# Attention scores of an MLA layer: from two to four column tiles with 32 keys each, turned by VectorE instead of TensorE

## What is computed

```python
q = rmsnorm(x @ wq_a.T + b) @ wq_b.T + b          # 16 heads, 128 + 64 (rope)
kv, k_pe = rmsnorm(...), rope(...)                # one latent key/value of 128, one rope key of 64, for all heads
scores = (q_nope @ wkv_b_k . kv + q_pe . k_pe) / sqrt(192)    # within a sequence of 64 tokens, causal
p = softmax(scores);  out = (p @ kv) @ wkv_b_v @ wo.T + b
```

## Time and profile before

| | us |
|---|---|
| median of 3 executions (1074.99 to 1075.48) | 1075.35 |
| span of the profiled execution, first to last instruction | 1073.7 |
| TensorE busy | 1052.0 (98%) |
| VectorE, ScalarE, GpSimd busy | 501.7, 340.6, 280.1 |
| granted TensorE clock, mean | 0.999 |

### The profile page before, as it was taken

One profiled execution on the slowest core, in us unless ns is written; L12 is line 12 of the kernel. 1 busy time (PEld: TensorE's weight loads), 2 busy tenths in 40 slices (PEclk: granted clock), 3 DMA queues, 4 the chain that ended last, 5 costly groups with the idle time before them and its releaser, 6 DMA issues.

```text
span 1073.7 us, 16794 instructions
## 1 busy us (share of the span) xinstructions
PE 1052.0 (98%) x6465; PEld 862.3 (80%) x6465; DVE 501.7 (47%) x914; ACT 340.6 (32%) x630; POOL 280.1 (26%) x329
## 2 busy tenths in 40 slices
PE   6999999999999999999999999999999999999997
PEld 3677786788888888888888888888888888888886
DVE  3666556545555544555555557442522251234114
ACT  3565545423222232123222234342222222223220
POOL 2433362321112111131111312232242123213412
PEclk9999999999999999999999999999999999999999
DMA  9999973200022000220013061600020002000101
GB/s 361 415 418 396 386 274 91 72 20 21 21 64 94 20 12 21 72 96 21 20 50 99 21 206 41 216 1 1 1 76 4 1 1 79 1 1 1 40 1 40
DMA packets 40755, 101.24 MB, mean 94 GB/s; under 512 B 6954, under 2 KB 11077, under 8 KB 36197
## 3 DMA queue, kind: packets, MB, share of 16 engines
q1 hardware_dynamic: 38948, 96.62, 25.3%
q10 hardware_dynamic: 1728, 3.54, 0.8%
HBM read 74.45 MB, written 17.30 MB: 85 GB/s over the span
## 4 chain that ended last, share of the span: by engine, by line
PE 96%; DVE 1%; issue 1%; DMA 1%; POOL 0%; ACT 0%; SPq 0%; DVEq 0%; POOLq 0%; ACTq 0%
PE b_z L44 8%; PE b_z L46 8%; PE b_z L45 8%; PE b_turn L44 5%; PE b_turn L46 4%; PE b_turn L45 4%; PE b_score L44 4%; PE b_score L46 4%; PE b_prob L46 4%; PE b_prob L44 4%; PE b_score L45 4%; PE b_prob L45 4%; PE b_read L46 4%; PE b_read L44 4%; PE b_read L45 4%; PE b_read L623 2%
## 5 line engine op out<-in xcount | busy, mean ns | idle before, releaser
L1516 POOL TENSOR_TENSOR f_hT_lo<-f_h,f_hT_hi 128x512 fp32r<-128x512 f32 x64 | 82.1, 1283 | 241.3 <-ACT f_hT_hi L1571 232.3
L1632 DVE TENSOR_TENSOR f_h<-f_h 128x512 f32<-128x512 f32 x64 | 45.4, 710 | 154.8 <-ACT f_h L1564 154.8
L816 POOL TENSOR_TENSOR m_sc<-m_sc,m_rs 128x1024 f32<-128x1024 f32 x16 | 30.5, 1908 | 248.5 <-DVE m_rs L979 248.5
L44 PE MATMUL b_z<-m_zT_lo,m_wq_hi 128*128 128x512 f32 x192 | 74.9, 390 | 0.3 <-issue 0.3
L46 PE MATMUL b_z<-m_zT_hi,m_wq_hi 128*128 128x512 f32 x192 | 74.7, 389 | 0.0
L45 PE MATMUL b_z<-m_zT_hi,m_wq_lo 128*128 128x512 f32 x192 | 74.7, 389 | 0.0
L987 DVE TENSOR_TENSOR m_x<-b_score,m_x 128x512 f32<-128x512 f32 x32 | 22.1, 691 | 97.3 <-PE b_score L46 97.3
L858 ACT ACTIVATE m_qT<-b_z,m_q_bias 128x512 f32<-128x512 f32 x64 | 44.1, 689 | 71.1 <-PE b_z L46 65.2
L806 POOL TENSOR_TENSOR m_qpe<-m_qpe,m_swapped 128x512 f32<-128x512 f32 x32 | 41.3, 1292 | 79.7 <-DMA m_swapped<-m_by_sin 79.7
L1571 ACT CAST f_hT_hi<-f_h 128x512 fp32r<-128x512 f32 x64 | 39.8, 622 | 52.4 <-DVE f_h L1632 52.4
L879 ACT ACTIVATE m_sc<-m_sc 128x512 f32<-128x512 f32 x32 | 20.2, 632 | 103.0 <-DVE m_sc L971 103.0
(11 more groups left out here) (280 smaller groups left out, 2863.9 us busy)
## 6 DMA issues: line engine op xcount, KB each, us to landing
x_ctx_in<-ctx_rows_dram SPq DMA_DIRECT2D x16, 1024.0 KB, 14.5
x_ctxT<-ctx_turned_dram SPq DMA_DIRECT2D x15, 1024.0 KB, 14.0
m_swapped<-m_by_sin SPq DMA_DIRECT2D x128, 64.0 KB, 2.0
m_raw<-attn_raw_dram SPq DMA_DIRECT2D x6, 768.0 KB, 10.6
m_z_in<-z_scratch SPq DMA_DIRECT2D x4, 1152.0 KB, 5.7
x_x_all<-x_dram SPq DMA_DIRECT2D x16, 256.0 KB, 14.7
m_x<-x_scratch SPq DMA_DIRECT2D x4, 1024.0 KB, 6.3
x_scratch<-m_x SPq DMA_DIRECT2D x4, 1024.0 KB, 4.3
```

The source lines that it names most:

```text
L44: nc.tensor.matmul(out, lh, rl, start=first, stop=False)
L816: q.tensor_tensor(e, e, rs[:].unsqueeze(2).broadcast_to([P, HB, SEQ]), ALU.mult).then_inc(s["normed"], 1)
L1516: q.tensor_tensor(hT_lo[k % 6][:], h[:, k % 2], hT_hi[k % 6][:].bitcast(F32), ALU.subtract).then_inc(s["h_lo"], 1)
L1632: v.tensor_tensor(h[:, k % 2], h[:, k % 2], h[:, k % 2], ALU.mult).then_inc(s["squared"], 1)
```

## The change

Scores are laid out with 32 keys on 32 partitions and four blocks of keys side by side: part c holds 2 sequences, its 128 tokens are cut in 4 tiles of 32. Bank b of the two score banks has one sequence of each part: block w = 0 is the first 32 queries on the first 32 keys, w = 1 the last 32 queries on the first keys, w = 2 the last on the last, so the quarter above the diagonal is no longer computed. A unit's scores are 128 x 768 instead of 128 x 1024. VectorE turns them with its own transpose of 32 x 32 blocks (`turn_scores`, `turn_probs`), TensorE's transposes go, and the mask is added after the turning, by GpSimd. Maximum and sum over 64 keys are now made of two blocks by two small instructions. `exp`, the copy of the probabilities and their split are one instruction each. The rope scores stand in two runs, the second behind `rope_half(u+1, 0)`. Token order changes with it: loads of z, loads and stores of x1 are 4 DMAs of 32 partitions where they were one.

```diff
     def load_z(sp, g):
-        sp.dma_start(z_in[:, :, 0:ZW], z_t[g]).then_inc(z_loaded, 16)
-        sp.dma_start(z_in[:, :, ZW:ZW + ROPE], z_t[g][:, :, QLR + KVLR:ZW]).then_inc(z_loaded, 16)
+        for c in range(PARTS):
+            sp.dma_start(z_in[part(c), :, 0:ZW], z_t[g, c]).then_inc(z_loaded, 16)
+            sp.dma_start(z_in[part(c), :, ZW:ZW + ROPE], z_t[g, c][:, :, QLR + KVLR:ZW]).then_inc(z_loaded, 16)
...
+        def mask(u):
+
+            pool.wait_ge(s["s_turned"], 2 * (u + 1))
+            own = sc[:].rearrange("p (b w n) -> p b w n", b=2, w=3)[:, :, 0::2]
+            q.tensor_tensor(own, own, causal[:].unsqueeze(1).unsqueeze(1).broadcast_to([P, 2, 2, HU * QB]),
+                            ALU.add).then_inc(s["masked"], 1)
...
         def slot(g, n, u):
             if runs(g, n, 1):
+                mask(u - 1)
+            rope_add(u, 0)
+            if runs(g, n, 1):
                 norm(u - 1)
-            rope_add(u)
+            rope_add(u, 1)
             if n == 1:
                 bias_x1(g)
...
         def exp(u):
 
-            for half in range(2):
-                act.wait_ge(s["shifted"], 2 * u + half + 1)
-                a.activation(sc[:, HALF * half:HALF * half + HALF], sc[:, HALF * half:HALF * half + HALF],
-                             ACT.Exp, scale=SCALE).then_inc(s["exped"], 1)
+            act.wait_ge(s["shifted"], u + 1)
+            a.activation(sc[:], sc[:], ACT.Exp, scale=SCALE).then_inc(s["exped"], 1)
...
+        def turn_scores(u):
 
             dve.wait_ge(s["scored"], u + 1)
...
+            for b in range(2):
+                v.transpose(sc[:, 3 * P * b:3 * P * b + 3 * P], b_s[b][:, 0:3 * P]).then_inc(s["s_turned"], 1)
+
+        def turn_probs(u):
+
+            dve.wait_ge(s["normed"], u + 1)
+            dve.wait_ge(s["pv"], u)
+            v.transpose(pT[:], sc[:]).then_inc(s["p_turned"], 1)
...
         def scores(g, u):
...
+            for b in range(2):
+                for k in range(2):
+                    for c in range(PARTS):
+                        t_.matmul(b_s[b][part(c), 2 * P * k:2 * P + P * k], keys_all[:, 0, 2 * b + k, c], queries(qT[:], b, k, c),
+                                  start=k == 0, stop=False)
+            rope_scores((0, 1)).then_inc(s["half_scored"], 1)
...
+        def rope_scores(heads):
+
+            for k in range(2):
+                for c in range(PARTS):
+                    for b, h in enumerate(heads):
+                        of = slice(SEQ * h, SEQ * h + SEQ)
+                        to = b_s[b][part(c), 0:3 * P].rearrange("p (w h n) -> p h w n", w=3, h=2)[:, h, 2 * k:2 + k]
+                        mm = t_.matmul(to, keys_all[of, 1, 2 * b + k, c], queries(qpe[of], b, k, c), start=False, stop=heads[0] == 1 and k == 1)
+            return mm
```

More of the change, by code:

```diff
@@ L795, in gpsimd @@
         pool.wait_ge(s["setup"], 1)
-        for half in range(2):
[L797 to L806, removed]
+        for c in range(PARTS):
+            rows = causal[part(c)].rearrange("p (h k) -> p h k", k=QB)
+            q.affine_select(out=rows, in_=rows, compare_op=ALU.is_ge, fill=-BIG, base=0,
+                            pattern=[[0, HU], [-1, QB]], channel_multiplier=1).then_inc(s["consts"], 1)
@@ L827, in groups @@
             slots(pool, slot)
-        return dict(groups=groups, rope_add=rope_add, norm=norm)
+        return dict(groups=groups, rope_add=rope_add, mask=mask, norm=norm)
     def scalar(act):
@@ L857, in q_part @@
             act.wait_ge(s["scored"], u)
-            a.activation(qT[:, h], b_q[h % 2][:], ACT.Identity,
+            a.activation(qT[:, 2 * (h % 2) + h // 2], b_q[h % 2][:], ACT.Identity,
                          bias=q_bias[:, HU * n + h:HU * n + h + 1]).then_inc(s["q_done"], 1)
         def probs(u):
[L862 to L865, removed]
+            act.wait_ge(s["p_turned"], u + 1)
+            act.wait_ge(s["pv"], u)
+            a.copy(pT_hi[:], pT[:]).then_inc(s["pT_hi"], 1)
         def out(u):
@@ L955, in mask @@
-        def mask(u):
+                split(of_part(oT_lo, c), b_o[c][:].rearrange("p (t h q) -> p t h q", t=T4, h=HU), of_part(oT_hi, c), s["oT_lo"])
+        def turn_scores(u):
             dve.wait_ge(s["scored"], u + 1)
[L958 to L961, removed]
@@ L1078, in rope_half @@
             for k in range(KQ):
+                if of is not None and k == KQ - 1:
+                    pe.wait_ge(s["half_scored"], of + 1)
                 mm = mm3(nc, b_r[m][:], (wq_hi[:, k, cols], wq_lo[:, k, cols]), (zT_hi[:, k], zT_lo[:, k]), k == 0, k == KQ - 1)
             mm.then_inc(s["rope_made"], 1)
-        def turn_scores(u):
-            pe.wait_ge(s["masked"], 2 * (u + 1))
-            for half in range(2):
-                turn(b_s[half], lambda k: sc[:, HALF * half + P * k:HALF * half + P * k + P], HB // 4).then_inc(s["s_turned"], 1)
         def q_unit(g, n, u):
@@ L1120, in project, with weigh @@
             mm.then_inc(s["projected"], 1)
-        def weigh(g, u, half, last=False):
+        def weigh(g, u, last=False):
             pe.wait_ge(s["kv_lo"], g + 1)
@@ L1195, in slot @@
                     pe.wait_ge(s["zq_lo"], T4 * (g + 2))
-                for half in range(2):
-                    weigh(before(1)[0], u - 1, half)
+                weigh(before(1)[0], u - 1)
             scores(g, u)
@@ L1202, in slot @@
             ahead = (g, n + 1) if n < 3 else (g + 1, 0)
-            rope_half(*ahead, u + 1, 0)
-            turn_scores(u)
+            rope_half(*ahead, u + 1, 0, u)
+            scores_end()
             rope_half(*ahead, u + 1, 1)
@@ L2065, in _ @@
             pe.wait_ge(F["s"]["xT_lo"], 4)
-            for half in range(2):
-                m["weigh"](G, U - 1, half)
+            m["weigh"](G, U - 1)
             m["scores"](G, U)
-            m["project"](2, U - 1, 0)
-            m["turn_scores"](U)
-            for i in range(1, 4):
+            m["project"](2, U - 1, 0, U)
+            m["scores_end"]()
+            for i in range(1, 3):
                 m["project"](2, U - 1, i)
             f["up"](0, 0)
-            m["turn_probs"](U)
             f["up"](0, 1)
-            m["weigh"](G, U, 0, last=True)
+            m["project"](2, U - 1, 3)
             pe.wait_ge(F["s"]["relu"], 2)
-            m["weigh"](G, U, 1, last=True)
+            m["weigh"](G, U, last=True)
             f["up"](0, 2)
```

215 lines of the change are left out of this document (109 added, 106 removed).

## The result

The changed kernel takes **1126.98 us** (median of 4 runs, 1124.36 to 1128.11), the kernel before 1075.41 beside it: a ratio of 1.0476, 95% interval [1.0461, 1.0491]. It is 4.8% slower; 1105 were forecast, 22 us too few. The profiled execution has a span of 1122.6 us, 48.9 more than the earlier trace rows.

What follows compares the result with a forecast made beforehand. TensorE bounds, busy 1052.0 of 1073.7 us. 1073.7 - 34 + 10 + 7 + 28 + 5 + 6 + 2 + 6 = 1103.7, with 1.7 around the span 1105 us, 2.8% slower; forecast 1088 to 1115 (64%), range 1088 to 1132.

Steps and rivals of the forecast that it cites:

- rival 2: TensorE: column tiles of 32 run only two at a time, 32 us, up to 1137; rivals 2 to 4 together 24%.
- rival 3: TensorE rope runs: short matmuls have a floor of 27 ns, 17 us, 1122; rivals 2 to 4 together 24%.
- rival 4: VectorE's transposes cost twice a pass, 13 to 16 us, 1120; rivals 2 to 4 together 24%.
- TensorE's saving, 16 units: Transposes 1.76 and latent scores 0.44 saved, rope scores 0.06 lost: 2.14 us a unit, 34 us.
- third head, ordinary units: TensorE's third head waits 1.25 us for the softmax chain and `q_part(0)`; 8 units, 10 us.
- third head, n=0 units: Split of new values adds 0.6 ahead of the chain: 1.85 us each in 4 units, 7 us.
- third head, three n=1 units: Groups 1 to 3: mask waits behind GpSimd's bias additions after the x1 reload; 9.2 us three times, 28 us.
- residuals (`x2_done`): Units n = 0: swap's DMAs behind eight z issues delay the first residual 2.4 us in two units, 5 us.
- late weight fill: Unit 0: third fill waits for a split behind the probabilities on VectorE, s + 23.3 against 17.3: 6 us.
- end of stage m: Where stage f is woven in, the same softmax chain costs about 2 us.
- clock: Matmuls behind long TensorE waits run at 1.2 GHz for a while: 1.5 us for each of 4, 6 us.
- rival 1: Reload does not hold the mask and the chain is cheaper: 1073 or 1065 us; 9% for faster, 3% within 0.2%.

Runs made afterwards that it cites:

- experiment 4: Kernel before, with the x2 store and the x1 reload each in four DMAs of 32 partitions in place of one; 1075.54 us, ratio 0.9999.
- experiment 7: Changed kernel with 52 matmuls that nobody reads put ahead of the third head's wait in each of three slots; 1119.08 us.
- experiment 3: Changed kernel with sums over keys and reciprocal ahead of the second half's rotation on VectorE again; 1115.77 us, ratio 1.0373.
- experiment 1: Changed kernel with the four bias additions to x1 one unit later in GpSimd's queue; 1089.85 us, ratio 1.0135.
- experiment 2: Changed kernel with the mask added by VectorE at the head of the shift, in place of GpSimd, bias additions left in place; 1100.14 us.
- experiment 8: Experiment 6 plus normalisation ahead of GpSimd's first-half rope addition and transposed probabilities ahead of VectorE's second-half rotation, last unit alike; 1051.18 us, ratio 0.9772.
- experiment 6: Changed kernel with the orders of experiment 1 and experiment 3, and the first query head evicted ahead of the exponential on ScalarE; 1069.33 us, ratio 0.9943.

## Why the forecast was right, and where it was short

The direction and the mechanisms that it priced held; sizes were off, and a cost that it set to nothing was there. The measured time lies above the 1088 to 1115 us to which the forecast gave 64%. It is inside the range up to 1132 only by the room left for rivals 2 to 4, none of which came true: so much of it is luck.

By term, in whole us of the profiled span: the forecast beside what was measured. Waits are taken from the start-to-start periods of the units, changed kernel against the kernel before, with the 2.2 us saved in each added back. So the sum comes out by construction; the split within a period goes by the waits and the clock in its rows.

| term | forecast | measured |
|---|---|---|
| TensorE's saving, 16 units | -34 | -35 |
| third head, ordinary units | +10 | +9 |
| third head, n=0 units | +7 | +7 |
| third head, three n=1 units | +28 | +37 |
| residuals (`x2_done`) | +5 | +8 |
| late weight fill | +6 | +7 |
| end of stage m | +2 | +5 |
| clock | +6 | +10 |
| step back of the group loop | 0 | +1 |
| sum | +30 | +49 |

**What TensorE saves**: right in each part, by the unit's first two microseconds and by the periods. Taking four tiles to cost per pass what two cost was the step that rivals 2 and 3 disputed.

**The ordinary unit's chain**: right, 1.1 to 1.3 us against 1.25. Transposes, mask (1.26), maximum, exponential (0.84) each came within 0.05 of their term.

**Unit n = 1**: the step that failed, by size. "That store and load are now four DMAs each I cost at nothing" was wrong, and the reason given for it too: the issues did not hide. The last of four stores is issued 1.75 us behind the first, and the reload, which waits for it, goes out that much later in experiment 4. In unit 9 store to addition went from 10.73 to 14.20 us; 9.2 + 3.5 is the 12.7 measured. Experiment 4 shows 2.3 of the 3.5 in a kernel that has nothing else of the change. The waits of groups 1 and 3 are 12.3 us, 3.1 over the forecast. In group 1 it is the same thing (10.57 to 13.82). In group 3 only half of it is (12.46 to 13.96): the kernel before was 1.7 us slower there than in unit 9, with its store issued at 576.17, and the forecast read unit 9 alone for all three. In all 10 us.

```profile
588.63 5.04 POOL L811 TENSOR_TENSOR m_x<-m_x,m_wo_b 128x512 f32<-128x512 f32 x4 [20.58 <-DMA m_x<-x_scratch]
```

**Units n = 0**: in the slot behind unit 4's scores (308.70) the rotation can start after 17.4 us, forecast at 16 to 17, and the residual starts after 24.7 and ends after 25.4, where the forecast had its end at 24.7:

```profile
326.06 0.75 DVE L952 SCALAR_TENSOR_TENSOR m_by_sin<-b_read,m_rope_bias,m_sin 128x512 f32<-128x512 f32 x1 [6.04 <-DMA m_swapped<-m_by_sin]
...
333.38 0.68 DVE L1015 TENSOR_TENSOR m_x<-b_score,m_x 128x512 f32<-128x512 f32 x1
```

So it costs 3.0 in two units, not 2.4, and 1.3 ahead of group 3, where I expected none since it loads no z. The end of stage m shows waits of 2.0 and 1.6 in the rows; from the last scores to the end of the span it took 437.9 us against 435.4, with 2.2 of saving in it, so 5 in all. Which work fills the last us of that was not tried.

**Clock**: the 4 falls at 1.5 us were in truth six: three long waits (5 us, by experiment 7), the two of 3 us (1.6 each, measured for one by experiment 3), the weight fill (an estimate of 1.6, half of its 3.2 us at half clock). My step "three of the new waits, and perhaps the 6 us one" left out the two waits of 3 us, behind which it fell too. It does not fall behind every wait of 3 us: the last section has the cases.

**Rivals**: 1 fell with the rows of unit 9, and experiments 1 and 2 show its converse (without the mask behind the reload, 37 and 27 us are back). 2, 3 and 4 fell with three groups of rows.

The 1.3 us at the loop's step is open. The row is `issue`: 1.6 us at 424.17, ahead of the first head behind unit 7's scores, where the kernel before has 0.3. It is there in experiment 8 too, and no run varied it.

## What to carry to other kernels

When work moves from the engine that bounds the kernel to another engine's queue, look at what already stands in that queue ahead of it and what that waits for: here one mask behind four additions that waited for a DMA cost 37 us with its share of the clock, more than the whole saving, and moving the additions one slot gave it back. A change that removes slack from the critical engine has to be timed together with the orders that the old slack allowed; the change alone was 4.8% slower, with four orders changed as well 2.3% faster. And a transfer cut into four parts is to be costed by the end of the last part: 2.3 us here for a store and the reload that waits for it.

## What was not expected of the hardware

- 32 matmul records on eight tiles of 64 rows and 32 columns start 11 ns apart on average; two neighbours of one pass stand 6 to 10 ns apart in the trace.
- Behind the wait of 3.0 us that ended at 334.20 the clock was at first still at 2.4 GHz and fell to 1.2 GHz only when matmuls ran again (mean 0.64 over the next 4.7 us of unbroken work). Behind the long waits it was down when work resumed. A wait of 3 us does not always bring it down: in experiment 6 one of 3.03 us ended at 447.58 and in experiment 7 one of 2.99 at 333.50, and the clock stayed at 1.00 over the next 8 us and more; in experiment 1 the clock was at 0.50 as soon as a wait of 2.77 us had ended (334.28).
- Filling a wait with matmuls that nobody reads makes the kernel faster (experiment 7) without shortening the wait that was filled (23.67 and 23.62 us from scores to third head).
